# A two-layer decoder on one core: slots that begin in a stagger, expert weights loaded ahead of their rows, and joins that SyncE is given later

## The reference, cut to what matters

```python
x = LN(x + L0_attn(x))          # decayed linear scan over the tokens, then a projection
x = LN(x + L0_xattn(x, ctx))    # 16 heads of 16, rotary embedding, softmax
x = LN(x + L0_ffn(x))           # weights AND activations rounded to a 4-bit grid, 256 -> 704 -> 256
x = LN(x + L1_attn(x))          # linear attention and a GELU block, 256 -> 1024 -> 256
x = LN(x + L1_xattn(x, ctx))    # softmax attention again
x = LN(x + L1_ffn(x))           # 8 experts, the best 2 of each token, 256 -> 512 -> 256
```

## Time and profile before

| | us |
|---|---|
| median of 3 runs (1042.85 to 1046.83) | 1045.75 |
| the profiled execution | 1051.46 |
| its span on the core | 1049.5 |
| TensorE matmuls busy, 87% of the span | 915.3 |
| VectorE busy, 61% | 641.6 |
| ScalarE busy, 43% | 449.3 |
| GpSimd busy, 26% | 277.1 |
| TensorE's granted clock, mean over the span | 0.933 |

### The profile page before, as it was taken

The page is one execution under the profiler, slowest core; times in us unless marked ns, Lnnn a source line. Parts: engine busy times, 40 slices in busy tenths (PEclk is TensorE's granted clock), DMA queues, the critical chain, the costliest instruction groups (busy, mean ns, idle before and its releaser), DMA issues.

```text
span 1049.5 us, 20142 instructions
## 1 busy us (share of the span) xinstructions
PE 915.3 (87%) x7498; PEld 731.0 (70%) x7498; DVE 641.6 (61%) x1909; ACT 449.3 (43%) x1096; POOL 277.1 (26%) x416
## 2 busy tenths in 40 slices
PE   6677979999989997989999989989999997598980
PEld 5366646799767666657788667767877886487970
DVE  6996799752457986898544685987544632024006
ACT  3154633244435444535353535564435543143440
POOL 5720113221104542113121322432211232023222
PEclk9787989999969987999999979999999999699995
DMA  9998000010001000000000014214201277888944
GB/s 321 388 330 281 2 1 0 1 31 11 21 12 33 31 31 21 2 1 11 6 17 16 16 32 137 72 41 144 95 1 56 75 225 254 305 294 323 404 177 160
DMA packets 39425, 114.88 MB, mean 109 GB/s; under 512 B 5464, under 2 KB 21600, under 8 KB 38688
## 3 DMA queue, kind: packets, MB, share of 16 engines
q1 hardware_dynamic: 35584, 103.35, 28.6%
q0 software_dynamic: 3744, 10.24, 2.6%
HBM read 99.13 MB, written 37.59 MB: 130 GB/s over the span
## 4 chain that ended last, share of the span: by engine, by line
PE 57%; DVE 27%; issue 6%; DMA 5%; ACT 3%; SPq 2%; POOL 0%; another core or an unknown queue 0%; POOLq 0%; DVEq 0%; ACTq 0%
PE ps L689 39%; PE ps L694 6%; PE ps L701 6%; DVE PT L1094 3%; PE ps L765 3%; DMA EW<-moe_w 2%; DVE stat L1029 1%; DVE PT L1054 1%; DMA xs_d<-X,idx 1%; DVE sm L1045 1%; DVE PT L1049 1%; PE ps L832 1%; DVE PT L1053 1%; ACT PT L1413 1%; DVE slot_rows L1040 1%
## 5 line engine op out<-in xcount | busy, mean ns | idle before, releaser
L1584 POOL TENSOR_TENSOR stat<-stat,mhalf 128x1 f32<-128x1 f32 x112 | 66.6, 595 | 360.8 <-DVE stat L1031 360.7
L689 PE MATMUL ps<-wall,slot_rows 128*128 128x256 f32 (+1 forms) x448 | 134.1, 427 | 6.5 <-ACT KB L1440 4.4
L689 PEld LDWEIGHTS ps<-wall,slot_rows 128*128 128x128 f32 x448 | 81.0, 196 | 30.9 <-issue 19.8
L701 PE MATMUL ps<-KB 16*128 16x128 f32 (+1 forms) x2048 | 85.2, 309 | 19.7 <-ACT PT L1413 5.8
L701 PEld LDWEIGHTS ps<-KB 16*128 16x128 f32 (+1 forms) x2048 | 72.7, 210 | 38.8 <-issue 29.0
L1094 DVE TENSOR_REDUCE PT<-ps 128x8 f32<-128x1024 f32 x64 | 75.3, 1220 | 33.2 <-PE ps L701 30.1
L689 PE MATMUL ps<-wgu,slot_rows 128*128 128x352 f32 x256 | 84.2, 481 | 7.8 <-DVE KB L1156 3.4
L694 PE MATMUL ps<-cst,PT 128*128 128x128 f32 x512 | 78.0, 295 | 11.0 <-DVE PT L1094 8.8
L694 PEld LDWEIGHTS ps<-cst,PT 128*128 128x128 f32 x512 | 63.1, 152 | 23.4 <-DVE PT L1094 9.7
L689 PE MATMUL ps<-work,EW 128*128 128x128 f32 x480 | 61.2, 281 | 20.2 <-DMA EW<-moe_w 20.2
L689 PE MATMUL ps<-slot_rows,wall 128*128 128x128 f32 x640 | 76.8, 276 | 0.3 <-ACT slot_rows L1430 0.3
(11 more groups left out here) (221 smaller groups left out, 1815.0 us busy)
## 6 DMA issues: line engine op xcount, KB each, us to landing
EW<-moe_w SPq DMA_DIRECT2D x30, 514.0 KB
EW<-moe_w SPq DMA_DIRECT2D x30, 512.0 KB
PT<-moe_w SPq DMA_DIRECT2D x12, 514.0 KB
PT<-moe_w SPq DMA_DIRECT2D x12, 512.0 KB, 7.8
wall<-wts SPq DMA_DIRECT2D x1, 4104.0 KB, 21.1
work<-xs_d SPq DMA_DIRECT2D x31, 128.5 KB
slot_rows<-ys_d SPq DMA_DIRECT2D x8, 384.0 KB, 6.2
KB<-ys_d SPq DMA_DIRECT2D x8, 384.0 KB, 6.8
```

What stands on the lines that cost most here:

```text
L689: last = k.e.matmul(o, a, b, start=(i == 0), stop=(i == len(pairs) - 1))
L701: last = k.e.matmul(ps[:, at, c * P:(c + 1) * P], lhsT[lane, c * P:(c + 1) * P], rhs[lane, c * P:(c + 1) * P], start=True, stop=True)
L1584: return k.e.tensor_tensor(v[:, 7:8], v[:, 8:9], mhalf[:, :], ALU.pow)
```

## The change

Three edits, all in the planner's description of the work; no instruction is added, and none does anything else than before. The instructions of all engines are the same in number and kind.

1. `plan_sample`: the first piece of samples 1 to 5 (the scan) now also needs the event `(n - 1, "xT", 0)`, at which the sample before has its rows turned for the first attention. So samples 1 to 5 are planned to begin one behind the other.
2. `early_turns`: the loads of tiles 23 to 26, in buffers that are free from the start, are listed with all weights first (up and down of 23, 24, 25, 26) and then the rows (23, 24, 25). Before, each tile's rows came ahead of its weights.
3. `plan_join`: for batch 0 alone the planner is told of a delay of 6.0 ahead of SyncE's fetch and of 10.0 ahead of its write of the output. The delays exist only in the plan: they move these issues back in SyncE's order.

```diff
@@ plan_sample
-    yield piece(work=[("D", 0.72, None), ("A", 0.7, None)], needs=[(n, "x")], alone=n < NS)
+    yield piece(work=[("D", 0.72, None), ("A", 0.7, None)], needs=[(n, "x"), *[(n - 1, "xT", 0)] * (0 < n < NS)],
+                alone=n < NS)
@@ early_turns
-    for x in range(NT):
-        yield from ((what, x) for what in ("rows", "load up", "load down") if early(what, x))
+    for kinds in (("load up", "load down"), ("rows",)):
+        yield from ((what, x) for x in range(NT) for what in kinds if early(what, x))
@@ plan_join
     for what, n in join_turns():
+
+        early_one = batch_of(n) < len(BATCHES) - 1
         if what == "fetch":
-            yield piece(work=[("S", 0.5, None), ("Q", 1.1, None), ("L", 2.4, (n, "fetched"))], alone=True,
+            yield piece(work=[*[("L", 6.0, None)] * early_one, ("S", 0.5, None), ("Q", 1.1, None), ("L", 2.4, (n, "fetched"))],
+                        alone=True,
                         needs=[(n, "saved"), ("table", len(BATCHES) - 1),
...
         else:
-            yield piece(work=[("D", 0.41, None), ("S", 0.5, None), ("Q", 0.4, None), ("L", 2.0, (n, "out"))], needs=[(n, "last root")],
-                        alone=True)
+            yield piece(work=[("D", 0.41, None), *[("L", 10.0, None)] * early_one, ("S", 0.5, None), ("Q", 0.4, None),
+                              ("L", 2.0, (n, "out"))], needs=[(n, "last root")], alone=True)
```

## The result

The changed kernel takes 1033.9 us (median of 5 runs, 1032.66 to 1037.21) against 1045.75 before (5 runs, 1042.85 to 1046.84): a ratio of 0.9898, 95% interval 0.9872 to 0.9924. It is faster by 11.9 us, a third of the 35 forecast. The profiled execution has a span of 1032.5 us (1034.37 with what lies around it), 17.0 less than that of before, which was one of the longer ones.

What follows compares the result with a forecast made beforehand. TensorE, busy 915.3 of 1049.5 us, was taken as the bound, with idle time and half clock to win. Tail 16, start 0 and second turn 19 gave 35 us, 1045.75 to 1011; range 995 to 1036.

Steps and rivals of the forecast that it cites:

- The stagger, second turn, 19 us: 281 to 497 us: evened VectorE work cuts TensorE's idle and clock cost from 40.8 to 21.6 us, 19 won.
- the prediction's sign of being wrong: 300 to 500 us: the prediction is wrong if TensorE's idle time there stays at 20 us.
- 19 + 0: The stagger's two terms: 19 us won in the second turn, 0 at the start.
- 592 to 640 us, put at nothing: Stretch of the last four samples: no gain taken, as they had been spread before; bound 11 us.
- The rival of single chains: Second turn: waits within each sample, which a stagger doesn't shorten, so only the tail pays; 1030 us, chance 0.16.
- The start, 0 (-15 to +10): 0 to 127 us: VectorE's smaller lead and TensorE's earlier need cancel; 0 us taken, between -15 and +10.
- up to 16.5 us: First 127 us, clock 0.87: by the skill's clock rule, a TensorE with less to do could lose this much.
- The early loads, 8.3 + 1.5: Tail, weights ahead of rows: TensorE idles 7.8 instead of 16.1 us, and a later 2.0 falls to about 0.5.
- only the stagger pays: Tail: early weights still fill the queues, so TensorE's wait only moves from tile 19 to 21; 1021 us, chance 0.08.
- The joins, 4 + 2: Tail, batch 0's joins later on SyncE: the 4.0 us wait for tile 32's rows goes, with about 2 of half clock.
- the tail alone at half its price: Upper end of the forecast range, given as 1036 us.

Runs made afterwards that it cites:

- e4: The changed kernel with Silu and both Gelu replaced by Relu, leaving one table load of 55: 1008.81 us, ratio 0.9649 to the kernel before.
- e1: The kernel before with the stagger of samples 1 to 5 alone, without the two tail edits: 1033.44 us, ratio 0.9887.
- e3: The kernel before the change with Silu and both Gelu replaced by Relu, leaving one table load of 24: 1034.45 us, ratio 0.9892.
- e5: The changed kernel with batch 0's joins also planned 60 us later on VectorE, behind the last batch's turns: 1028.77 us, ratio 0.9845.
- e15: The changed kernel with joins later on VectorE and Silu worked out through Tanh, with 32 more VectorE operations: 1028.31 us, ratio 0.9827.
- e9: The changed kernel with Silu alone replaced by Relu, Gelu kept, 29 table loads: 1024.57 us, ratio 0.9787.

## Why the prediction was wrong

**The bound was read right, and one engine was left out of it.** Idle time and half clock are what the change could win, and TensorE's busy total fell by 12.8 us with the clock. But ScalarE was nowhere in the argument; its row was passed over at 43%.

**The stagger, second turn, 19 us: the size failed through a cost that was never counted.** "No instruction is added, so it is worth only what TensorE idles less" is the sentence that failed: 31 instructions are added, though none by the diff. VectorE's share evened out, as the prediction says, and from 281 to 497 us 27.9 us stayed where 21.6 were forecast; without loads (e4) it is 22.8. What fell there is mostly the clock's part, from 18.9 to 9.9 us; idle time went from 21.9 to 18.0, and between 300 and 500 us, where the prediction's sign of being wrong was that it stays at 20, from 18.5 to 18.0: by that sign too the step failed. Net, e1 has 11.8 us for the whole stagger. Gross, without loads on either side, it is 25.4 us for the whole change (e3, e4), of which the tail's edits, measured on their own, are some 3: about 22 for start and turns together, give or take 5. The loads take 15 of them back. That 22 lies near the 19 + 0 is luck in part, since it did not come from the stretch that was priced alone: 592 to 640 us, put at nothing "the four last samples having been spread before", gave 9.4 us in the profile of the change, nearly the bound of 11, and 183 to 281 and 497 to 592 us took 6.3 back (idle 4.9 for 0.3 and 3.2 for 1.5). The rival of single chains had the right kind of mechanism, latency on another engine between two products of one sample, but for the wrong reason: it held the chains to be as long as before, and they became longer.

**The start, 0 (-15 to +10).** The first use of a gate/up product is at 97.33 us, 122.31 before and near 95 forecast, and the start did not starve:

```profile
97.33 0.52 DVE L1160 TENSOR_TENSOR KB<-KB,ps 128x352 f32<-128x352 f32 x1
```

In 0 to 127 us TensorE idles 39.3 us, 5.8 more than before; in 127 to 183 us 4.9, 4.6 less, and at clock 1.00 instead of 0.94. Together that is 2 us won, near 0 as said. The clock over the first 127 us is 0.87 as before, so that the up to 16.5 us which the prediction feared there were not taken.

**The early loads, 8.3 + 1.5: the landing was mis-sized.** Counted from the ranking, SyncE came as forecast within 2.5 us: early weights at +10.0 (forecast 8), rows at +17.6 (15.3), `load up 21` at +21.5 (20). It lands at +30.0, not 24.5: 8.5 us, where the prediction took 4.5, as "now most of these are through". They were not: it had the weights landed by +19 at 404 GB/s, but that rate held up to 895 us, +30, because the loads of tiles 19 to 22 and the rows share it. TensorE's waits there fell from 16.09 + 1.96 to 1.23 + 11.29 + 0.42 us, 5.1 and not 9.8. Of that, some 1.5 us go again, as two pairs of products behind these waits run slow and not one. That the wait moves from tile 19 to tile 21 was a part of the rival "only the stagger pays".

**The joins, 4 + 2: the wait moved instead of going.** The prediction did look at tile 34 and gave it 2.5 us of slack (`place` at 958 to 960, TensorE at 962.5). Both come sooner, with the fetch at 919.58: `place` at +23.3 and TensorE at +23.1, no slack. What was left out is that rows are still to be sent and to land behind the `place`, 0.9 + 2.3 us. Four waits of 6.7 us in all took the place of the one of 4.0. e5, which moves the joins on VectorE too, has none of them and wins 5.5 us.

**Summed.** 35 forecast; 17.0 in the profiled span, 14.2 ahead of the last ranking and 2.8 behind it. The 5.1 of the loads less the 2.7 of the joins is 2.4, near the 2.8, though slow products and some short waits are not in it. The prediction's range has a slip: the tail alone at half its price is 1045.75 - 8 = 1038, and not 1036; 1033.9 lies inside either way. Not settled: how the 15 us that the loads cost are spread over the stretches (the profiled execution of e3 took 8 us less than its median, so that its stretches say little), and why VectorE's added work in e15 costs about as much as the loads that it replaced.

## What to carry to other kernels

Before pricing a reordering, compare the instructions of every engine in both orders, not only those that look busy: state that an engine holds between instructions (here ScalarE's table) turns a mere change of order into added work, at 1.28 us of ScalarE and about 0.48 us of the total each. When a transfer is moved ahead of another, ask first whether the DMA engines are full in that stretch; here they were, and the wait moved from tile 19 to tile 21 and kept most of its length. And a rule that saves such switches by reordering must be weighed against what the old order overlapped: here 30 loads fewer, worth 14 us, came with an order that cost some 86.

## What had not been expected of the hardware

- A table load takes 1283 ns each time, with 0.01 us between its end and the activation behind it, and 0.3 us of idle time in sum ahead of the 16 at Silu. Exp, Silu and Gelu each needed a load behind either of the others. Tanh behind Exp needed none: 29 loads in e15, as many as with Relu in e9.
- The kernel's time paid 0.48 us (0.41 to 0.55) for each load of 1.283 in the order with 55; 0.49 (0.32 to 0.66) in the one with 24 and 0.34 (0.10 to 0.58) in the one with 25 agree with it.
- In the tail 16 DMA engines together moved 380 to 406 GB/s with their busy share at 1.00 to 1.03; a weights load that took 8.5 us to land there took 5.1 when 2 MB less stood ahead of it.
